# Sampling coordinates spread by DMA in fp32 instead of by matmuls, and image rows made three at a time, in an attention and deformable-convolution kernel

## The reference

```python
om = conv3x3(x, w_off) + b_off                    # 27 channels
off_y, off_x, mask = om[:, :9], om[:, 9:18], sigmoid(om[:, 18:])
py = off_y + row + ky                             # where tap k of each output pixel samples
px = off_x + column + kx
y0, x0 = floor(py), floor(px);  wy, wx = py - y0, px - x0
# bilinear: four neighbours, zero outside the image
sampled = v00*(1-wy)*(1-wx) + v01*(1-wy)*wx + v10*wy*(1-wx) + v11*wy*wx
sampled = sampled * mask
out = einsum("bckhw,ock->bohw", sampled, w) + b
out = batch_norm(out) * gamma + beta
return relu(out) + x
```

## Time and profile before

| | us |
|---|---|
| median of 3 runs | 1183.15 |
| lowest and highest | 1178.95, 1183.35 |
| the profiled execution, its own time | 1181.56 |
| its span, first to last instruction | 1179.8 |

### The profile page before, as it was taken

The page is one execution under the profiler, slowest core; times in us unless marked ns, Lnnn a source line. Parts: engine busy times, 40 slices in busy tenths (PEclk is TensorE's granted clock), DMA queues, the critical chain, the costliest instruction groups (busy, mean ns, idle before and its releaser), DMA issues.

```text
span 1179.8 us, 26432 instructions
## 1 busy us (share of the span) xinstructions
PE 1079.9 (92%) x7562; PEld 824.4 (70%) x7562; DVE 864.1 (73%) x1037; ACT 810.5 (69%) x1496; POOL 551.9 (47%) x432
## 2 busy tenths in 40 slices
PE   4778888789996799999999999999999999999983
PEld 2435555433445688888878888878888888888873
DVE  2379999843436377777777777777777778888885
ACT  1347767511122688888878888888888888888865
POOL 1028788342232144555555445544554455555540
PEclk9689999999998899999999999999999999999996
DMA  3000000043211100000000000000000000000001
GB/s 121 0 1 1 0 0 0 1 92 82 57 45 43 18 10 12 14 10 9 12 15 12 9 10 14 11 11 11 15 11 9 10 10 3 4 4 2 2 3 71
DMA packets 53391, 22.51 MB, mean 19 GB/s; under 512 B 44750, under 2 KB 51412, under 8 KB 53076
## 3 DMA queue, kind: packets, MB, share of 16 engines
q1 hardware_dynamic: 52924, 21.46, 7.5%
q10 hardware_dynamic: 408, 0.25, 0.1%
HBM read 10.25 MB, written 7.01 MB: 15 GB/s over the span
## 4 chain that ended last, share of the span: by engine, by line
PE 80%; DVE 10%; issue 6%; ACT 1%; DMA 1%; DVEq 1%; POOL 1%; ACTq 0%; POOLq 0%
PE PS L1157 79%; DVE region L672 2%; DVE region L628 2%; DMA bcol<-in_boff 1%; DVE region L632 1%; DVE region L647 1%; DVE region L634 1%; PE PS L1227 1%; DVE region L617 1%; DVE region L629 1%; PE PS L1425 0%; DVE region L785 0%; DVE two L880 0%; DVE region L614 0%; ACT region L1151 0%
## 5 line engine op out<-in xcount | busy, mean ns | idle before, releaser
L1157 PE MATMUL PS<-region 128*128 (+4 forms) x5504 | 717.0, 294 | 17.7 <-POOL region L436 7.3
L1157 PEld LDWEIGHTS PS<-region 128*128 128x128 f32 (+1 forms) x5504 | 629.6, 182 | 109.6 <-issue 78.8
L821 DVE TENSOR_TENSOR region<-PS,region 128x1296 f32<-128x1296 f32 x256 | 386.0, 1508 | 163.5 <-PE PS L1157 163.4
L525 POOL TENSOR_TENSOR region<-region 128x576 f32<-128x576 f32 x256 | 307.5, 1201 | 363.6 <-DVE region L821 363.6
L1077 ACT ACTIVATE region<-x 64x576 f32<-64x576 f32 x512 | 349.1, 682 | 30.2 <-ACT x L1073 0.8
L1073 ACT ACTIVATE x<-PS,cst 128x640 f32<-128x640 f32 x256 | 202.3, 790 | 89.1 <-PE PS L1157 88.9
L833 DVE TENSOR_REDUCE region<-region 128x720 f32 (+1 forms) x256 | 228.6, 893 | 2.8 <-POOL region L525 2.8
L1157 PE MATMUL PS<-region,selb 6*128 6x320 bf16 (+1 forms) x512 | 106.5, 287 | 0.0
L1157 PE MATMUL PS<-region,woff 128*108 (+3 forms) x192 | 88.6, 605 | 0.8 <-DVE xp L750 0.8
L431 POOL TENSOR_TENSOR region<-region,cst 128x1024 f32<-128x1024 f32 x32 | 61.6, 1926 | 49.8 <-ACT region L953 25.3
L672 DVE SCALAR_TENSOR_TENSOR region<-region,wr (+4 forms) x57 | 73.9, 1297 | 0.1
(11 more groups left out here) (136 smaller groups left out, 802.4 us busy)
## 6 DMA issues: line engine op xcount, KB each, us to landing
two<-xr_scratch SPq DMA_DIRECT2D x300, 16.0 KB, 1.7
xr_scratch<-region SPq DMA_DIRECT2D x8, 384.0 KB
region<-xp SPq DMA_DIRECT2D x10, 264.0 KB, 4.4
out<-region SPq DMA_DIRECT2D x4, 512.0 KB, 3.0
px_scratch<-region SPq DMA_DIRECT2D x64, 27.0 KB
region<-px_scratch SPq DMA_DIRECT2D x64, 27.0 KB
region<-xp SPq DMA_DIRECT2D x6, 280.5 KB, 4.5
x<-in_x SPq DMA_DIRECT2D x1, 1536.0 KB, 10.7
```

The lines of the kernel that those rows point to most:

```text
L525: pool.tensor_tensor(uu[:, r % 4, :, 0:FOLD], uu[:, r % 4, :, 0:FOLD], uu[:, r % 4, :, NA - FOLD:NA], ALU.add).then_inc(fold_ready, 1)
L821: v.tensor_tensor(uu[:, u4].rearrange("p o (b a) -> p b o a", b=3), PS[:, 3 * u:3 * u + 3, 0:432].rearrange("p b (a o) -> p b o a", o=C), ...
L1157: return nc.tensor.matmul(o, l, r, start=start, stop=stop)
```

## The change

Coordinates. The x coordinates are no longer split in three. SP stores them in fp32 straight from `two` to `px_scratch`, laid out as (image, row, tap, column), 256 bytes for each row and tap. In the stream, `load_px` loads two rows at a time with every partition of an image receiving the same 4,608 bytes: the source address has a step of zero over 64 partitions. Two DMAs of 64 x 1152 fp32 (295 KB of written SBUF each) fill two lines of a ring of 8 lines (`PXR`) in SBUF; each pair of lines has its own semaphore. ACT takes Abs in place in SBUF (128 x 576) and the Relu read from there. The two `selb` matmuls of each row, `selb` itself with its CAST, and the four instructions of each chunk that split the coordinates (ACT L1059, POOL L471, DVE L785 and L787) are gone.

Image rows. The 8 rows of a chunk are made in rounds of 3, 3 and 2, before the taps of rows 0, 3 and 6; the rounds take PSUM banks 6 and 7 in turn, and ACT evicts a round with one instruction after rows 2, 5 and 7 (128 x 432 or 128 x 288).

Order and waits. ACT no longer waits for PE's `px` but for a load. DVE waits before it writes `two` for the store of two chunks before, and before the first two steps of the image stage for the stores of chunks 6 and 7. SP starts the stream with four pairs of loads, then the split image rows. In a chunk SP loads the split image rows first, then two lines of coordinates each time that ACT has used them.

The diff, cut to its core:

```diff
-        px_dram = nc.dram_tensor("px_scratch", (B, 3, KK, HW), BF16, kind="Internal").ap()
+        px_dram = nc.dram_tensor("px_scratch", (B, H, KK, W), F32, kind="Internal").ap()
...
-        sx = sxf.bitcast(BF16)[0:6, :].rearrange("p (k r c) -> p k r c", k=KK, c=W)
+        px = sxf.rearrange("p (r a) -> p r a", r=PXR)
...
-                    sp.wait_ge(lo_ready, done(n))
+                    sp.wait_ge(om_out, done(n, 2))
                     for b in range(B):
                         row, h = OC * (b % PAIRS) + KK, b // PAIRS
-                        sp.dma_start(px_dram[b, :, :, bass.ds(n * CH, CH)].rearrange("s k c -> k s c"),
-                                     spl[row:row + KK, u, :, h * CH:(h + 1) * CH]).then_inc(px_stored[u], 16)
+                        sp.dma_start(px_dram[b, bass.ds(n * RPC, RPC)].rearrange("r k c -> k r c"),
+                                     two[row:row + KK, u, h * CH:(h + 1) * CH].rearrange("p (r c) -> p r c", c=W)).then_inc(px_stored[u], 16)
...
-            def load_px(m, g, chunk):
+            def load_px(g, y, line):
 
                 for h in range(2):
-                    sp.dma_start(sx[3 * h:3 * h + 3, :, RPC * (chunk % 2):RPC * (chunk % 2 + 1), :].rearrange("p k r c -> p k (r c)"),
-                                 px_dram[bass.ds(g + h * PAIRS, 1), :, :, chunk * CH:(chunk + 1) * CH].rearrange("b s k c -> (b s) k c")).then_inc(px_in, 16)
-                sp.wait_ge(px_in, 32 * m + 32)
-                sp.sem_inc(px_ready, 1)
+                    sp.dma_start(px[W * h:W * (h + 1), line:line + GR, :].rearrange("p r a -> p (r a)"),
+                                 px_dram[bass.ds(g + h * PAIRS, 1), bass.ds(y, GR)].rearrange("b r k c -> b (r k c)").to_broadcast([W, GR * KK * W])
+                                 ).then_inc(px_in[line // GR], 16)
...
+                def chunk(g, c, rows, after):
+                    s = g * NCH + c
+                    if rows:
+                        sp.wait_ge(slot_ready, 3 * s + 2)
+                        load_rows(s + 1, g + 1, c, c % 2)
+                    if after is not None:
+                        for line in range(0, RPC, GR):
+                            sp.wait_ge(wt_ready, done(s * RPC + line + GR - 1, 2))
+                            load_px(after[0], after[1] * RPC + line, line)
...
-                    pool.tensor_tensor(rest, two[0:PAIRS * OC, u, :], spl[0:PAIRS * OC, u, 0, :], ALU.subtract).then_inc(rest_ready, 1)
...
-            v.tensor_copy(selb[:, :], two[0:6, 0, 0:P]).then_inc(bd_ready, 1)
...
-                    v.tensor_copy(spl[0:PAIRS * OC, u, 1, :], rest).then_inc(mid_ready, 1)
-                    v.tensor_tensor(spl[0:PAIRS * OC, u, 2, :], rest, spl[0:PAIRS * OC, u, 1, :], ALU.subtract).then_inc(lo_ready, 1)
...
+            dve.wait_ge(px_done, done(NCH - 2))
             stage(0, 0)
+            dve.wait_ge(px_done, done(NCH - 1))
             stage(1, 1)
...
-                    a.activation(spl[0:PAIRS * OC, u, 0, :], two[0:PAIRS * OC, u, :], ACT.Copy).then_inc(hi_ready, 1)
...
-                act.wait_ge(bc_ready, done(n))
-                a.activation(ab[:, u, :].rearrange("p (b a) -> p b a", b=2), PS[:, 6:8, 0:PXA], ACT.Abs, bias=c_("negx")).then_inc(ab_ready, 1)
+                if line % GR == 0:
+                    act.wait_ge(px_in[line // GR], 32 * loads)
+                a.activation(px[:, line, :], px[:, line, :], ACT.Abs, bias=c_("negx")).then_inc(ab_ready, 1)
...
+            def slots_out(q, slot, b, bank):
+
+                act.wait_ge(slot_ready, done(q))
+                act.sem_inc(act_turn, 1)
+                a.activation(img4[:, :, bass.ds(slot, ROUNDS[b]), :].rearrange("p k r o -> p r k o"),
+                             PS[:, bank, 0:KK * C * ROUNDS[b]].rearrange("p (r k o) -> p r k o", k=KK, o=C), ACT.Copy).then_inc(row_out, 1)
...
-            def px(n, line, image=None, before=False):
-                mm(PS[:, 6, 0:PXA], selb[:, :], sx[:, 0:5, line, :])
-                mm(PS[:, 7, 0:PXB], selb[:, :], sx[:, 5:KK, line, :]).then_inc(bc_ready, 1)
+            def slot_round(q, b, u, bank):
+
+                pe.wait_ge(row_out, free(q))
+                for r in range(3 * b, 3 * b + ROUNDS[b]):
                     for h in range(2):
-                        mm(PS[W * h:W * (h + 1), 7, PXB:PXB + KK * C], xrow[:, image[0], image[1], h, :], wsp[0:SPLITS * C, :])
+                        at = KK * C * (r - 3 * b)
+                        ins = mm(PS[W * h:W * (h + 1), bank, at:at + KK * C], xrow[:, u, r, h, :], wsp[0:SPLITS * C, :])
+                ins.then_inc(slot_ready, 1)
...
+                            if here and r in (0, 3, 6):
+                                if r == 0:
+                                    pe.wait_ge(xr_ready, s + 1)
+                                slot_round(3 * s + r // 3, r // 3, 1 - u, 6 + (u + r // 3) % 2)
                             taps(n, c * RPC + r, r % 2, None)
```

More of the change, by code:

```diff
@@ L127, in build @@
         woff = sb("woff", [P, 6, PAIRS * OC])
-        selb = sb("selb", [6, P], BF16)
+        selw = sb("selw", [P, 3])
         two = sb("two", [P, 2, 2 * CH])
@@ L1110, in chunk @@
                         for r in range(RPC):
-                            slot = TOP + H - RPC + r if first else None if last else c * RPC + (TOP - RPC + r)
-                            row(s * RPC + r, r % 2, slot)
+                            row(s * RPC + r, r, s + 1, r % 2)
+                            if r in (2, 5, 7) and (first or not last):
+                                b = (2, 5, 7).index(r)
+                                slots_out(3 * s + b, (TOP + H - RPC if first else c * RPC + TOP - RPC) + 3 * b, b, 6 + (u + b) % 2)
                             if r in (4, 6) and not (last and end):
```

119 lines of the change are left out of this document (38 added, 81 removed).

## The result

After the change the kernel takes 1075.49 us, median of 4 runs (1073.90 to 1076.04); the kernel before took 1181.05, median of 4 (1178.94 to 1183.35). The ratio is 0.910, 95% interval 0.908 to 0.913. The profiled execution took 1075.3 us, its span is 1073.5.

What follows compares the result with a forecast made beforehand. The prediction took PE to bound the stream: 63.4 us from three pairs with images, 21.1 from the last pair, 6 from transitions and 0.8 at the start, 91.3 off 1181.56, gave 1090 us, range 1077 to 1116.

Steps and rivals of the forecast that it cites:

- PE bounds the stream, and what leaves its queue shortens it until another engine takes over: Stream: PE has no gap, so removing the coordinate matmuls saves 0.35 us of PE in each of 256 rows.
- Taps 2.40: PE in the stream: the tap matmuls of one row take 2.40 us of the 2.93 us period.
- ACT at 20.1 us a chunk, 2.51 a row: ACT in chunks with images: Abs, Relus, hats and evictions sum to 20.1 us, 2.51 a row against PE's 2.60.
- Period 2.60 and 2.42: Stream after the change: 2.60 us a row with images and 2.42 in the last pair, set by PE.
- The rival that ACT takes over, 1096: Stream: with Abs at 0.79 us ACT needs 2.62 us a row, 2.46 in the last pair; 1096 us, chance 0.14.
- Three pairs, 63.4: Stream, three pairs with images: 192 rows each 0.33 us shorter, 63.4 us in all.
- Start, 0.8: Start of the kernel: without the CAST of `selb`, 0.8 us is saved.
- Offset stage and transitions, 6: Nothing gained inside the offset stage; its end and the start of the stream together gain 6 us, bounds 4 and 7.5.
- DMA hidden, SP with 6 us of slack: Coordinate loads in the stream: they stay hidden at 113 GB/s, landing 6 us before ACT wants them.
- slow source: Rival, coordinate loads: reading one source repeatedly at 88 GB/s makes a chunk 28.3 us and the kernel 1342; chance 0.12.
- SP's queue: Rival, stream: load issues of 1.38 us make SP take 2.70 us a row in three pairs; 1110 us, chance 0.10.
- Three engines stalling by turns: Rival, stream: engines within 0.3 us of one another stall, 2.75 and 2.55 us a row; 1127 us, chance 0.07.

Runs made afterwards that it cites:

- e9: The changed kernel with image rows made one at a time, each evicted a row later (row 7 has two evictions): 1096.4 us, ratio 0.925.
- e2: The changed kernel with Abs on only 16 of its 576 elements, computing wrong values: 1032.9 us, ratio 0.872.
- e5: e2 also without the stream's image matmuls and their evictions, computing wrong values: 1002.1 us, ratio 0.847.
- e1: The changed kernel with Abs without its per-partition bias, computing wrong values: 1053.9 us, ratio 0.889.
- e8: The changed kernel with the old 6 x 128 selector DMA and its CAST to bf16 restored at the start, result unused: 1079.6 us, ratio 0.913.
- e11: The changed kernel with the old 6 x 128 selector DMA restored at the start, without the CAST: 1077.05 us, ratio 0.910.
- e4: The changed kernel with coordinate loads reading 64 different rows of the input instead of one row 64 times, computing wrong values: 1075.3 us, ratio 0.908.
- e3: The changed kernel with image rows made one at a time, each evicted after ACT's weights for the same row: 1139.75 us, ratio 0.961.

## Why the prediction was right or wrong

The sum was 15 us short: 3.6 at the start, 0.7 at the transitions, 9.2 in the three pairs with images and 1.5 in the last. Some steps were wrong without showing there, since their errors nearly cancelled.

- **PE bounds the stream, and what leaves its queue shortens it until another engine takes over.** Right. The coordinates alone gave 85 us (e9). But another engine did take over: ACT, to which the forecast had given 0.14.
- **Taps 2.40.** The step that failed first. 0.2 of the 2.40 is not taps but is paid once for each unbroken block. I had seen that five changes of kind go and put them at 5 x 0.02 at most, where it is 5 x 0.2 a chunk with images and nearly all 8 in the last pair, and then charged 0.02 a row the other way for the weight load. The image matmuls were mis-sized too: 8 x 0.18 = 1.44 us a chunk in the forecast, 0.30 + 0.30 + 0.22 = 0.82 in rounds. 1.0 + 0.6 + 0.2 is the difference between 20.8 and 19.0: PE needs 19.1 us a chunk (e2), and no more than 2.22 a row without images (e5).
- **ACT at 20.1 us a chunk, 2.51 a row.** Too low by 0.5: 8 x 0.03 for the Abs (0.81 until the Relu, not 0.78) and 0.3 for the evictions (1.55, not 1.25). The 1.25 was the length of three evictions back to back in the image stage (377.56), of 0.53, 0.52 and 0.42 us, each starting 0.1 before the one ahead ends; in the stream they stand alone, and the Abs behind starts 0.02 to 0.03 after their end. The Abs itself was short by 0.09, since its nearest row had no bias operand (e1), while the wait on its result was charged 0.1 and shows 0.03. ACT was the next engine, with 2.57 a row, and set the period.
- **Period 2.60 and 2.42.** Measured 2.57 and 2.38 (2.41 with the last pair's first chunk, which still makes image rows). That it came so near was luck: PE's too long taps and ACT's too short chunk nearly met. The slack that I worked out between them (PE doesn't stall) was wrong: PE waits for ACT 58 times in the profile.
- **The rival that ACT takes over, 1096.** Its mechanism is what happened; gaps of ACT and PE traded places as it said. Its price was too high: 2.62 a row from an Abs of 0.79 with 0.89 until the Relu, measured 0.77 and 0.81. The Trainium skill, VectorE: DVE Perf Modes, section on the TRN2 errata, had been set against the row of 743 ns. Compared like with like, both with a bias column, 640 elements from PSUM take 790 ns here and 576 from SBUF 772: 64 fewer elements gain 18 ns, not the 54 at the slope of (1256 - 772) / 576 = 0.84 ns an element. The 36 ns that are missing are near the page's 52 cycles, 43 ns at the 1.2 GHz that it gives for ScalarE. The trace agrees with the rule, and I should have kept it.
- **Three pairs, 63.4.** 72.6: about 5 for 2.57 instead of 2.60, and 3.2 that was in no term. In the kernel before PE stands still for 1.63 us at the start of the second pair (592.23) and for 1.61 at that of the third (781.57), with nothing to wait for in the profile; at the fourth it doesn't. After the change a chunk takes 20.59 us across these seams as elsewhere, and PE's longest gap there is 0.59. That PE's slack now hides the seam is argued, not tried. The period was read inside a pair, and the sum left the seams out. The rest, under 1 us, I did not trace.
- **Start, 0.8.** The CAST was sized right. That with another DMA in place of the selector's the first loads land 3 us earlier was not in the sum: I weighed only the CAST. The trace has 4.4 us less ahead of the last offset chunk, but neither e8 and e11 nor the scatter of the first stage let me say how much of it the change made.
- **Offset stage and transitions, 6.** Right: 6.7. The short CAST at 360.54 lies beside POOL's memsets, and the first taps wait for `load_rows` (5.63 us), not for coordinates. First taps were forecast near 396 and came at 390.90, by the start and by `load_rows` issued already at 382.84.
- **DMA hidden, SP with 6 us of slack.** Right: share 0.52 within the 0.3 to 0.6, landing 4.2 us, and ACT waits for no load. The first lines of a chunk, the ones that the 6 us were worked out for, had landed 6.9 us before ACT took them in the median of the chunks, the least of all loads 2.6. Neither the slow source (e4) nor SP's queue showed.
- **Three engines stalling by turns.** It didn't happen in this kernel. In e3 two of them, ACT and PE, do just that, for 43 us, because the eviction stands in the wrong place.
- **The range.** Its low end had transitions of 7.5 and rows of 2.56; with 21.1 and 0.8 these give 1181.6 - 100.4 = 1081, not the 1077 that I wrote. The start beyond 0.8 us and the seams, 3.6 and 3.2 us, were in neither end.

## What to carry to other kernels

A floor read from a row without gaps still holds what the neighbours cause; measure an engine's need from blocks of two lengths, and compare an instruction only with rows of the same operands, bias included. When the bound leaves an engine, sum the in-order queue of the next one over a whole loop, extras and all. Place an instruction that waits for the other engine's newest work a row behind it: its place alone was worth 43 us here.

## What was not expected of the hardware

- A break in a run of fp32 matmuls, by a change to bf16 or by a wait, costs PE 0.2 us here: blocks of 18, 36 and 54 took 2.47, 4.68 and 6.88 us, and taking out three breaks a chunk with their image matmuls gave 1.28 us (e5 against e2).
- The bias column costs ACT 92 ns an instruction (772 against 680).
- With a DMA of 128 x 12 bytes in place of 6 x 512 bytes at the start, and three columns fewer in the constants, the first loads landed 3 us earlier (9.56 against 12.5). The load issued behind it took SP 0.99 us instead of 0.35 to issue; whether that is the cause was not tried, and the gain was not clear in the time.
- 64 partitions reading the same 4.6 KB cost no more than 64 different rows (share 0.52 at 123 GB/s against 0.54 at 125, e4).
